# Second bank pair for a batch's exponentials, lengths carried in the constants, Newton refinement in two steps, length scale applied in the exponential

## The reference

```python
def _layernorm(x, axis=-1, eps=1e-05):
    m = jnp.mean(x, axis=axis, keepdims=True)
    v = jnp.var(x, axis=axis, keepdims=True)
    return (x - m) / jnp.sqrt(v + eps)
# attention over the feature axis: 8 heads of 16 rows, 256 queries, 256 keys
s = SCALE * jnp.log(k_length.astype(jnp.float32))[:, None, None, None]
attn = jnp.einsum('bhdq,bhdk->bhqk', qh, kh)
attn = jax.nn.softmax(s * attn, axis=-1)
out = jnp.einsum('bhqk,bhdk->bhdq', attn, vh)
# feed-forward, two experts of 1024 hidden units, top one chosen by a router
h = jnp.einsum('nd,ehd->enh', x_flat, w_fc)
a = jnp.square(jnp.where(h >= 0, h, 0.5 * h))
expert_out = jnp.einsum('enh,edh->end', a, w_proj)
out = jnp.einsum('end,en->nd', expert_out, mask * top_weight[None, :])
# x = x + attention(layernorm(x), ctx, ctx, k_length); x = x + ffn(layernorm(x))
```

## Time and profile before

| | us |
|---|---|
| median of 3 runs | 180.46 |
| lowest, highest | 179.83, 181.18 |
| the profiled execution | 181.36 |
| its span, first to last instruction | 179.5 |

### The profile page before, as it was taken

The page is one execution under the profiler, slowest core; times in us unless marked ns, Lnnn a source line. Parts: engine busy times, 40 slices in busy tenths (PEclk is TensorE's granted clock), DMA queues, the critical chain, the costliest instruction groups (busy, mean ns, idle before and its releaser), DMA issues.

```text
span 179.5 us, 4124 instructions
## 1 busy us (share of the span) xinstructions
PE 164.6 (92%) x1522; PEld 142.8 (80%) x1522; DVE 127.0 (71%) x314; ACT 93.2 (52%) x179; POOL 57.9 (32%) x66
## 2 busy tenths in 40 slices
PE   2967898868899999999999999999999999999990
PEld 2855655547599869869898899979879999999990
DVE  6679789896999787889988837669239449336311
ACT  4251867943847557954367344453681563433400
POOL 6023804600024932141454232202231616443210
PEclk9999999996999999999999999999999999999997
DMA  3787776672147026005000550000001000010001
GB/s 110 237 281 241 236 242 213 200 228 88 58 159 244 15 88 221 19 29 175 4 0 2 179 177 0 5 0 4 0 29 33 0 0 4 0 58 0 0 4 58
DMA packets 18499, 16.32 MB, mean 91 GB/s; under 512 B 1840, under 2 KB 18352, under 8 KB 18480
## 3 DMA queue, kind: packets, MB, share of 16 engines
q1 hardware_dynamic: 17616, 15.28, 26.2%
q10 hardware_dynamic: 864, 0.79, 1.4%
HBM read 8.72 MB, written 1.05 MB: 54 GB/s over the span
## 4 chain that ended last, share of the span: by engine, by line
PE 74%; SPq 8%; DMA 8%; DVE 4%; issue 2%; ACT 2%; ACTq 0%; DVEq 0%
PE ops L1254 27%; PE hp L1236 24%; PE stp L1194 6%; PE pv L1214 6%; PE snp L1165 5%; PE stp L1198 4%; DMA q_st<-q_lo 4%; SPq L162 3%; DVE negm L729 3%; DMA x_raw<-x 2%; SPq L170 2%; DMA q_st<-q_hi 2%; PE ops L1172 1%; ACT probs L438 1%; SPq L139 1%
## 5 line engine op out<-in xcount | busy, mean ns | idle before, releaser
L324 POOL TENSOR_TENSOR a_buf<-l_buf 128x512 f32<-128x512 f32 x32 | 35.1, 1100 | 87.4 <-ACT l_buf L446 65.4
L438 ACT ACTIVATE probs<-stp 128x1024 f32<-128x1024 f32 x32 | 32.8, 1026 | 26.1 <-PE stp L1198 26.1
L729 DVE TENSOR_REDUCE negm<-snp 128x4 f32<-128x1024 f32 x28 | 34.2, 1221 | 15.8 <-PE snp L1165 15.8
L1236 PE MATMUL hp<-xt_hi,wfc_hi 128*128 128x256 f32 x128 | 37.6, 294 | 0.0
L1236 PE MATMUL hp<-xt_hi,wfc_lo 128*128 128x256 f32 x128 | 35.9, 281 | 0.0
L1236 PE MATMUL hp<-xt_lo,wfc_hi 128*128 128x256 f32 x128 | 35.9, 280 | 0.0
L827 DVE TENSOR_TENSOR a_lo<-a_buf,a_hi 128x512 fp32r<-128x512 f32 x32 | 23.6, 746 | 12.8 <-ACT a_hi L453 8.1
L446 ACT ACTIVATE l_buf<-hp 128x512 f32<-128x512 f32 x32 | 18.9, 594 | 18.2 <-PE hp L1236 18.2
L1254 PE MATMUL ops<-wproj_hi,a_hi 128*128 128x256 f32 x128 | 27.1, 293 | 0.0
L1236 PEld LDWEIGHTS hp<-xt_hi,wfc_hi 128*128 128x128 f32 x128 | 24.1, 189 | 2.9 <-issue 1.6
L1254 PE MATMUL ops<-wproj_hi,a_lo 128*128 128x256 f32 x128 | 25.7, 283 | 0.0
(11 more groups left out here) (78 smaller groups left out, 226.2 us busy)
## 6 DMA issues: line engine op xcount, KB each, us to landing
k_st<-k_hi SPq DMA_DIRECT2D x16, 128.0 KB, 2.4
wfc_raw<-w_fc_t SPq DMA_DIRECT2D x8, 256.0 KB, 3.4
wproj_raw<-w_proj_t SPq DMA_DIRECT2D x8, 256.0 KB, 3.0
q_st<-q_hi SPq DMA_DIRECT2D x14, 128.0 KB, 2.3
x_raw<-x SPq DMA_DIRECT2D x8, 128.0 KB, 2.6
v_raw<-ctx_t SPq DMA_DIRECT2D x8, 128.0 KB, 2.9
k_st<-k_lo SPq DMA_DIRECT2D x8, 128.0 KB, 2.2
q_st<-q_lo SPq DMA_DIRECT2D x8, 128.0 KB, 2.3
```

The lines of the kernel that those rows point to most:

```text
L324: pool.tensor_tensor(a_buf[d % 2][:, :, :], l_buf[d % 2][:, :, :], l_buf[d % 2][:, :, :], ALU.mult).then_inc(s_a, 1)
L438: act.activation(probs[g][:, :, :, :], stp[:, :, :].rearrange("p e (c n) -> p e c n", c=KC), ACT.Exp).then_inc(s_exp, 1)
L729: dve.tensor_reduce(negm[b % 2][:, :, :, g].rearrange("p c e -> p e c"), pair[:, :, :].rearrange("p e (c n) -> p e c n", c=KC), AX.X, ALU. ...
L1236: last = pe.matmul(hp[:, d % 2, half], wfc[w][:, kc, c * P:(c + 1) * P], xt[:, kc, :], start=(c % 2 == 0 and kc == 0 and w == 0 and xt is ...
```

## The change

Four edits.

1. In batch 1, kq(1,0) and kq(1,2) write `hp` and exp(1,0) and exp(1,2) read it; kq(1,1) and kq(1,3) stay with `stp`. The wait of kq(1,g) for exponentials goes back by one for g = 1 to 3. The fill(3) behind kq(1,0) is gone.
2. The lengths come as 8 more columns of the constants (as bits), and the constants are loaded by ScalarE's queue in the place of the lengths. SyncE's list has no load of constants any more.
3. The variance is kept as -0.5 (var + eps), the logarithm takes -2 as its scale, and the refinement is two steps: n1 = rs * rs * var', sc = (n1 + 1.5) * rs.
4. The score scale is no longer in `xsc`; `exp` reads column b of `scale_b` as its scale. exp(0,0) waits for it.

```diff
-        cst = sb("cst", [P, P + PAIRS])
+        cst = sb("cst", [P, P + PAIRS + B])
-        len_i = sb("len_i", [P, B], i32)
...
-            def load_consts():
-                sp.dma_start(cst[:, :], consts).then_inc(s_cst, 16)
-
             load_x(sp, 0)
             load_x(sp, 1)
             load_v(0)
-            load_consts()
             stack_k(sp, 0, 0)
...
-            def load_len():
-                act.dma_start(len_i[:, :], k_len.partition_broadcast(P)).then_inc(s_len, 16)
+            def load_consts():
+                act.dma_start(cst[:, :], consts).then_inc(s_cst, 16)
...
-                act.activation(xln[b % 2][:, :], xvar[b % 2][:, :], ACT.Ln).then_inc(s_xln, 1)
+                act.activation(xln[b % 2][:, :], xvar[b % 2][:, :], ACT.Ln, scale=-2.0).then_inc(s_xln, 1)
...
             def exp(b, g):
+                if b == 0 and g == 0:
+                    act.wait_ge(s_scale, 1)
                 act.wait_ge(s_st, PAIRS * b + g + 1)
                 wait(act, s_pv, b * 2 - 1 if g < PAIRS // 2 else b * 2)
-                act.activation(probs[g][:, :, :, :], stp[:, :, :].rearrange("p e (c n) -> p e c n", c=KC),
-                               ACT.Exp).then_inc(s_exp, 1)
+                act.activation(probs[g][:, :, :, :], (hp if b == 1 and g % 2 == 0 else stp)[:, :, :].rearrange("p e (c n) -> p e c n", c=KC),
+                               ACT.Exp, scale=scale_b[:, b:b + 1]).then_inc(s_exp, 1)
...
-                    dve.tensor_scalar(var[:, :], mv[:, 1:2], EPS, None, ALU.add).then_inc(s_var_, 1)
+                    dve.tensor_scalar(var[:, :], mv[:, 1:2], EPS, -0.5, ALU.add, ALU.mult).then_inc(s_var_, 1)
...
-                elif stage == 1:
+                else:
                     dve.wait_ge(s_n1_, b + 1)
-                    dve.tensor_scalar(n2[:, :], n1[:, :], -0.5, 1.5, ALU.mult, ALU.add).then_inc(s_n2_, 1)
-                else:
-                    dve.wait_ge(s_n2_, b + 1)
-                    dve.scalar_tensor_tensor(sc[:, :], n2[:, :], extra, rs[:, :], ALU.mult, ALU.mult).then_inc(s_sc_, 1)
+                    dve.scalar_tensor_tensor(sc[:, :], n1[:, :], 1.5, rs[:, :], ALU.add, ALU.mult).then_inc(s_sc_, 1)
...
             def len_float():
-                dve.wait_ge(s_len, 16)
-                dve.tensor_copy(len_f[:, :], len_i[:, :]).then_inc(s_lenf, 1)
+                dve.wait_ge(s_cst, 16)
+                dve.tensor_copy(len_f[:, :], cst[:, P + PAIRS:P + PAIRS + B].bitcast(i32)).then_inc(s_lenf, 1)
...
-                wait(pe, s_exp, PAIRS * b + g)
+                pair = hp if b == 1 and g % 2 == 0 else stp
+                wait(pe, s_exp, PAIRS * b + g - (1 if b == 1 and g > 0 else 0))
...
             scores_kq(1, 0)
-            fill(3)
             scores_kq(1, 1)
```

More of the change, by code:

```diff
@@ L22, with build @@
 PIECES = 8
-def build(nc, x, ctx_kv, ctx_t, k_len, w_router, w_fc_t, w_proj_t, consts, out):
+def build(nc, x, ctx_kv, ctx_t, w_router, w_fc_t, w_proj_t, consts, out):
     f32, f32r, i32 = mybir.dt.float32, mybir.dt.float32r, mybir.dt.int32
@@ L70, in build @@
         xst, xmv, xvar = two("xst", [P, 6]), two("xmv", [P, 2]), two("xvar", [P, 1])
-        xln, xrs, xn1, xn2, xsc = (two(n, [P, 1]) for n in ("xln", "xrs", "xn1", "xn2", "xsc"))
+        xln, xrs, xn1, xsc = (two(n, [P, 1]) for n in ("xln", "xrs", "xn1", "xsc"))
         q_f = two("q_f", [P, DIM])
@@ L85, in build @@
         yst, ymv, yvar = two("yst", [P, 6]), two("ymv", [P, 2]), two("yvar", [P, 1])
-        yln, yrs, yn1, yn2, ysc = (two(n, [P, 1]) for n in ("yln", "yrs", "yn1", "yn2", "ysc"))
+        yln, yrs, yn1, ysc = (two(n, [P, 1]) for n in ("yln", "yrs", "yn1", "ysc"))
         dot_out = sb("dot_out", [P, DIM])
@@ L109, in build @@
         s_kzero, s_qzero, s_nmzero, s_vones = sems("k_stack_zeroed"), sems("q_stack_zeroed"), sem("nm_zeroed"), sem("v_one_filled")
-        s_xst, s_xmv, s_xvar, s_xln, s_xrs, s_xn1, s_xn2, s_xsc = (
-            sem(n) for n in ("x_stats", "x_moments", "x_var", "x_ln", "x_rstd0", "x_newton1", "x_newton2", "x_scale"))
+        s_xst, s_xmv, s_xvar, s_xln, s_xrs, s_xn1, s_xsc = (
+            sem(n) for n in ("x_stats", "x_moments", "x_var", "x_ln", "x_rstd0", "x_newton", "x_scale"))
         s_qf, s_qhi, s_qlo, s_khi, s_klo = (sem(n) for n in ("q_f", "q_hi", "q_lo", "k_hi", "k_lo"))
@@ L118, in build @@
             sem(n) for n in ("pv_done", "pv_turned", "den_inverse", "attn_turned", "attn_out", "x2_ready"))
-        s_yst, s_ymv, s_yvar, s_yln, s_yrs, s_yn1, s_yn2, s_ysc = (
-            sem(n) for n in ("y_stats", "y_moments", "y_var", "y_ln", "y_rstd0", "y_newton1", "y_newton2", "y_scale"))
+        s_yst, s_ymv, s_yvar, s_yln, s_yrs, s_yn1, s_ysc = (
+            sem(n) for n in ("y_stats", "y_moments", "y_var", "y_ln", "y_rstd0", "y_newton", "y_scale"))
         s_x2n, s_logit = sem("x2n_ready"), sem("logit_ready")
@@ L422, in y_ln @@
                 act.wait_ge(s_yvar, b + 1)
-                act.activation(yln[b % 2][:, :], yvar[b % 2][:, :], ACT.Ln).then_inc(s_yln, 1)
+                act.activation(yln[b % 2][:, :], yvar[b % 2][:, :], ACT.Ln, scale=-2.0).then_inc(s_yln, 1)
             def y_rstd(b):
@@ L690, in x_newton @@
                 j = b % 2
-                if stage == 2:
-                    dve.wait_ge(s_scale, 1)
-                newton(stage, b, xvar[j], xrs[j], xn1[j], xn2[j], xsc[j], scale_b[:, b:b + 1], s_xrs, s_xn1, s_xn2, s_xsc)
+                newton(stage, b, xvar[j], xrs[j], xn1[j], xsc[j], s_xrs, s_xn1, s_xsc)
             def q_normalise(b):
@@ L778, in x2_newton @@
                 j = b % 2
-                newton(stage, b, yvar[j], yrs[j], yn1[j], yn2[j], ysc[j], 1.0, s_yrs, s_yn1, s_yn2, s_ysc)
+                newton(stage, b, yvar[j], yrs[j], yn1[j], ysc[j], s_yrs, s_yn1, s_ysc)
             def x2_normalise(b):
@@ L1013, in _ @@
             coefs(0)
-            x2_newton(3, 2)
             row_max(5, 1)
@@ L1193, in scores_kq @@
                         rows = slice(HALF * e, HALF * e + HALF)
-                        pe.matmul(stp[:, e, kc * DIM:(kc + 1) * DIM], k_st[j][rows, g, kc * P:(kc + 1) * P], q_st[j][rows, g, :],
+                        pe.matmul(pair[:, e, kc * DIM:(kc + 1) * DIM], k_st[j][rows, g, kc * P:(kc + 1) * P], q_st[j][rows, g, :],
                                   start=(kc == 0), stop=False, skip_group_check=True)
@@ L1197, in scores_kq @@
                         rows = slice(HALF * e, HALF * e + HALF)
-                        last = pe.matmul(stp[:, e, kc * DIM:(kc + 1) * DIM], pick[rows, g, :], mx[j][rows, :],
+                        last = pe.matmul(pair[:, e, kc * DIM:(kc + 1) * DIM], pick[rows, g, :], mx[j][rows, :],
                                          start=False, stop=True, skip_group_check=True)
```

27 lines of the change are left out of this document (6 added, 21 removed).

## The result

| | before | changed |
|---|---|---|
| median of 20 runs of each, us | 180.74 | 179.53 |
| lowest, highest | 179.31, 184.61 | 178.07, 184.05 |
| ratio, with its 95% interval | | 0.9939 (0.9913 to 0.9966) |
| the profiled execution | 181.36 | 178.59 |
| its span | 179.5 | 176.8 |

By the medians the change is 1.21 us, 0.7%, in its favour: within 1%, as forecast, but four times the 0.31 us of the sum. The forecast 180.15 lies 0.62 us above the measured median. So the change is worth 0.5 to 1.2 us, depending on the measure.

What follows compares the result with a forecast made beforehand. The chain of waits before the feed-forward's first matmul at about 49.2 us bounds the kernel, TensorE being full afterwards; -0.26 + 0.12 - 0.17 = -0.31 us from the 180.46 median gives 180.15 us, range 178.9 to 181.9.

Steps and rivals of the forecast that it cites:

- the sum: Whole kernel: -0.26 + 0.12 - 0.17 = -0.31 us, giving 180.15 us from the 180.46 median.
- The frame: TensorE is full from about 49.2 us, so effects show only in when the feed-forward's first matmul arrives.
- Term 1: Start to q_f of batch 0: xsc no longer needs scale_b, q_f at 6.28 instead of 6.54, -0.26 us.
- Term 2: Scale operand lengthens each exponential by 58 ns; exp(0,2) and exp(2,2) on the chain pay, +0.12 us.
- the slack: Batch 0's exp(0,1): 0.12 us free before its TensorE reader, just filled by two times 58 ns.
- Term 3: Batch 1's bank pairs: kq(1,2) no longer waits for exp(1,1), 0.34 us behind qk(2,0) instead of 0.51, -0.17 us.
- The other two overlaps: Batch 1: kq(1,1) moves earlier but qk(2,0) still waits for DMAs; kq(1,3) had no bank wait; no gain.
- Keeps it: Chain behind q_f (q_hi, stacking, scores, row maxima) has no other arrival near, so passes on the start's gain, 0.26 us.
- The stretch after ffn1 unchanged: After the first feed-forward matmul TensorE is full and loses no work, so the stretch stays 126 us long.
- The clock rival: Removed filler leaves a 1.8 us TensorE pause; clock falls between 29 and 34 us, 1.4 us lost, 181.55; chance 0.25.
- The start gains more: Without the lengths' small-packet DMA, batch 1's x lands 0.4 us sooner: 179.7, or about 178.7; chance 0.17.

Runs made afterwards that it cites:

- e4_const_scale: Changed kernel with the constant 0.3 as the exponentials' scale instead of the column of lengths; 178.54 us median of 4 runs, ratio 0.9876.
- e1_consts_only: Kernel before with only the lengths moved into the constants; 179.90 us median of 10 runs, ratio 0.9929.
- e7_len_added: Changed kernel with the lengths' old DMA added again ahead of the constants, its result unread; 178.78 us in one execution.
- e3_scale_newton: Kernel before with only the two-step refinement and the scale in the exponential; 180.62 us median of 10 runs, ratio 0.9996.
- e2_banks_only: Kernel before with only batch 1's alternating bank pairs and the filler removed; four executions, 179.12, 181.83, 182.60 and 183.58 us.
- e6_guard: Changed kernel with filler in both TensorE pauses, before qk(2,0) and qk(3,0); 178.34 us median of 10 runs, ratio 0.9904.
- e12_guard_banks: Changed kernel with filler in both pauses and bank pairs alternating in batch 2 too; 178.21 us median of 7 runs, ratio 0.987.
- e9_changed_again: Changed kernel run again with no edit but a comment; 179.81 us median of 12 runs, ratio 0.9922.

## Why the prediction was right, and where its sum was short

**The frame held.** The gain arose before ffn1 for the larger part, the first stretch was bound by the chain that the prediction went through, and the median fell within 1% of before. The sum has no part in that last point: a range of 3 us holds 0.3 as it holds 1.2.

**Term 1** (-0.26) was -0.38. The order of the steps was right, the constants came in time, and xsc took the place it was given. Mis-sized was the distance from scale_b to q_f: I kept the 0.17 us that lay between scale_b and xsc (0.21 in the timeline, where scale_b starts at 6.07), which was the time of a dependent step; without the dependence it is 0.08. bn_stats to scale_b is 0.77 and 0.78 us, so all of the 0.38 lies behind scale_b, 0.47 before and 0.08 now.

**Term 2** (+0.12) was too small. An operand costs 88 to 89 ns, above the 58 that I took as the only row's price and as the upper bound. The first stacking DMA of SyncE is 13.30 us behind qk(0,0), before 13.04: 0.26 more. Of this, 0.05 is there before the first exponential starts (7.39 us behind qk(0,0), before 7.34; e4_const_scale, without the operand, has 7.39 too). From exp(0,0) to exp(0,3) it is 0.20, where three times 88 ns are 0.26, so the slack hid 0.06 us and not 0.12. And this is one pair of profiles: of the other two without the operand and without a fall up to there, e1_consts_only has 13.19 and e4_const_scale 13.55, because qk(1,2) waited for a row maximum in them. After qk(3,0) the operand costs another 0.17. The 20 exponentials that I took to run beside a full TensorE are not all free either: in the last stretch two matmuls of values start 0.35 us behind the one ahead of them, with a constant as the scale 0.26. The worth of taking the operand out, 0.25 us with the clock up, rests on two runs. The Trainium skill, "ScalarE: Activation LUTs", "What ACT_TABLE_LOAD costs", gives about 93 ns for each pointer operand; the trace agrees with 88 to 89. The bound from VectorE's tiny operations spoke of another engine and was not a bound here.

**Term 3** (-0.17) was -0.28. The 0.17 came for the reason given: kq(1,2) at 0.34 us behind qk(2,0). The other 0.11 lie between kq(1,2) and kq(1,3) (2.01 us before, 1.90 now), where the first pair of matmuls took 0.39 us and now takes 0.28. The other two overlaps paid nothing, as forecast: exp(1,1) is 0.82 us earlier and qk(2,0) waits for its DMA all the same. What the term left out is that edits 1 and 4 act on the same wait, and that it depends on the landing of a DMA: 0.11 to 0.51 us over three profiles.

**"Keeps it" did not hold in full.** The prediction let every gain of the start pass on to ffn1, with SyncE's stacking of batch 3 starting when kq(1,3) is done. It does start then, but how long it takes varies: from the first to the last of the six issues 4.6 to 6.0 us over the fourteen profiles, one issue lasting up to 2.00 us where 0.59 is usual. In e7_len_added 0.6 us lost at the start were gone at qk(3,0). So part of what is gained ahead of it can be lost there. One pair of profiles gives no share, and what lengthens the issue was not tested.

**"The stretch after ffn1 unchanged" is the step that came out wrong.** From ffn1 to the end of the span it took 129.67 to 129.84 us in the four kernels without edits 3 and 4, and 128.99 to 129.37 in nine of the ten with them; the tenth, e3_scale_newton, had 129.72 with a DMA wait of 0.65 in it. With TensorE's idle time taken out, the stretch from its first to its last matmul is 125.2 to 125.4 us without these edits and 124.5 to 124.9 with them, e3_scale_newton's included. The rows of the matmuls differ by 1 to 2 ns. TensorE's own instructions there are the same, and e4_const_scale has the short matmuls too (279 and 281 ns), so the scale operand of the exponentials is not the cause. What is left is VectorE's: a Newton step less for each normalisation, and no scale operand in xsc. That this is the cause was not tested by itself; why it should shorten matmuls stays open.

**The clock rival** (0.25) is real as a mechanism and wrong as a median. The fall behind the new pause was seen (e2_banks_only, e4_const_scale), and closing both pauses makes 14 of 17 executions up (e6_guard, e12_guard_banks), where in the changed kernel and its variants with the first pause open it is 25 of 55. But the kernel before is up in 26 of 69: it falls as often, at other places. So the rival's price does not appear in the difference of the medians. The Trainium skill, "TensorE: Matmul & The Clock Gate", "Why this matters for your kernels", asks for a longer pause before the clock goes down; here it went down behind pauses of 0.84 (e1_consts_only, at 40.6 us), 1.20, 1.44, 1.98 and 2.02 us, and at 19.3 us behind none over 0.5; it also stayed up behind 1.96 to 2.07 in five profiles. So the trace does not agree, and the pause's length alone does not decide.

**"The start gains more"** (0.17) gave the right side and the wrong cause. bn_stats started at 5.30, 5.27, 5.17 and 4.83 us with the old first DMAs and at 4.73 to 5.26 in the ten profiles with the constants in ScalarE's queue, e7_len_added's among them. The means, without the latter, differ by 0.13, which so few profiles do not separate; the 0.56 of the first comparison is mostly chance.

**What remains.** With the clock up, -0.38 (start), +0.43 (0.26 up to the stacking of batch 2 and 0.17 behind qk(3,0)), -0.28 (banks) and -0.56 (last stretch) give -0.79 of about -1.2. No profile of the kernel before is without a fall, so this sum is put together from stretches of different executions. The other 0.4 us are not assigned; the landing of x (0.13) and of the stacking DMAs (the stretch from qk(2,0) to qk(3,0) varied by 1.2 us over the profiles) are where they would lie. The parts alone, up against up, gave -0.28, -0.59 (one execution) and -0.21, together -1.08, which so few executions do not fix to better than some tenths.

## What to carry to other kernels

Price a step that stays in the queue but loses its dependence anew: two independent small operations start about 0.1 us apart here, dependent ones 0.17 to 0.26. Take the cost of an operand on ScalarE from ScalarE, and expect an extension of one instruction to be paid at each place where that instruction ends a wait. Before comparing two profiles, compare their clocks: one fall here is worth 0.9 to 1.2 us, as much as the whole change, and filler that ends before the DMA it waits beside cost nothing and made the changed kernel's times narrow. Before summing gains along a chain, look at how much each later stretch varies by itself: an overlap or a head start is worth only what the next DMA leaves of it.

## What the runs showed of the hardware that was not expected

- The granted clock falls from 2.4 to 1.2 GHz in about 6 of 10 executions of either kernel (43 of 69, 12 of 20). In seven of the fourteen profiles it fell at 19.5, 31, 33 or 41 us, in the other seven only in the last 2.1 us, if at all. It fell behind a pause of TensorE of 0.84 us and stayed up behind one of 2.07. The changed kernel's times follow in steps: medians of 178.7 where it is up, 179.8 to 179.9 at 0.984 to 0.990, and 182.3 below that.
- A column of SBUF as the scale of an exponential over 128 x 1024 elements costs 88 to 89 ns (1114 against 1025 and 1026).
- Matmuls of the same shapes and clock take 279 and 281 ns in one program and 281 and 283 in the other; in the other profiles 279 or 280 and 281 with edits 3 and 4, 280 or 281 and 282 or 283 without them. The last stretch is shorter by about half a microsecond.
- SyncE's issue of one and the same 128 KB stacking DMA lasted 0.59 us in some profiles and up to 2.00 in others (32.88 us, e9_changed_again).
- A DMA of 32 bytes to each partition ahead of others need not delay its neighbour: bn_stats of x started at 4.73 us with it and at 4.74 without it, in one profile of each; over all profiles it started between 4.73 and 5.30.
